# A graph network in one kernel: Householder reflections and bisection steps planned into other LSTM steps

## The reference, cut to what matters

```python
# layer 0: two graph convolutions, then LSTMs over windows of p = 1..4 nodes
h = relu(einsum('ts,bsh->bth', adj, x @ Wg0 + bg0))
h = relu(einsum('ts,bsh->bth', adj, h @ Wg1 + bg1))
for p in range(1, MAX_SKIP + 1):
    nw = Tv // p
    wins = h[:, :nw * p, :].reshape(Bv * nw, p, Hd)
    last = _lstm_last(Wih[p-1], Whh[p-1], bih[p-1], bhh[p-1], wins)
    h = h.at[:, arange(nw) * p + (p - 1), :].set(last.reshape(Bv, nw, Hd))
x = layernorm(x + h)
# layer 1: x -> normalised adjacency -> W1 -> batch norm -> relu -> W2 -> batch norm
# layer 2: attention over 512 edges
# layer 3: spectral, with the eigenvectors U of the normalised Laplacian of adj
_, U = eigh(L_norm)
out = relu(einsum('mn,bnd->bmd', U.T, x) @ W1 + b1) @ W2 + b2
x = layernorm(x + einsum('nm,bmd->bnd', U, out))
```

## Time and profile before

| what | value |
|---|---|
| median of 3 runs | 2091.99 us (2091.33 to 2092.39) |
| the profiled execution | 2091.33 us |
| its span, first to last instruction | 2089.5 us |
| mean granted clock of TensorE | 0.966 of full speed |
| busy: PE, DVE, ACT, POOL | 1948.3, 1493.8, 1144.0, 758.3 us |
| LSTMs: p = 1, 2, 3, 4 | about 228 to 398, 636, 920, 1222 us |

### The profile page before, as it was taken

How to read it: one execution, slowest core, us unless ns; L and a number is a source line. 1 busy time by engine, 2 the same in 40 slices (tenths; PEclk the granted TensorE clock), 3 DMA queues, 4 the chain that set the end, 5 groups by cost and what they waited for, 6 DMA issues and landing times. The chain is left out here.

```text
span 2089.5 us, 32693 instructions
## 1 busy us (share of the span) xinstructions
PE 1948.3 (93%) x11833; PEld 1651.2 (79%) x11833; DVE 1493.8 (71%) x3825; ACT 1144.0 (55%) x1803; POOL 758.3 (36%) x1924
## 2 busy tenths in 40 slices
PE   6999888999999999999999989989799899699996
PEld 6999766788889999988787778866599534469896
DVE  5676666666656677788888878968656489789675
ACT  2444565445444454543444447747567588556675
POOL 2333345443444555000000036646544000107675
PEclk8999998999999999999999999999899999899898
DMA  3110101000100000010000033202222000004022
GB/s 107 47 41 1 41 1 41 1 1 1 41 1 1 1 1 1 1 41 1 1 1 0 1 106 102 91 21 92 69 82 72 11 1 1 11 21 123 32 71 82
DMA packets 65631, 71.15 MB, mean 34 GB/s; under 512 B 3767, under 2 KB 63294, under 8 KB 65470
## 3 DMA queue, kind: packets, MB, share of 16 engines
q1 hardware_dynamic: 65470, 69.07, 10.3%
HBM read 43.90 MB, written 25.17 MB: 33 GB/s over the span
## 5 line engine op out<-in xcount | busy, mean ns | idle before, releaser
L1852 ACT ACTIVATE l_gates<-l_acc,l_b 128x512 f32<-128x512 f32 (+1 forms) x504 | 300.9, 633 | 92.4 <-PE l_acc L473 90.0
L1859 ACT ACTIVATE l_gates<-l_cell 128x512 f32<-128x512 f32 (+1 forms) x144 | 84.0, 583 | 249.8 <-DVE l_cell L1913 156.3
L471 PE MATMUL l_acc<-l_x_hi,l_w1x_hi 128*128 128x336 f32 (+1 forms) x544 | 190.5, 350 | 20.4 <-DVE l_x_lo L1822 12.4
L1812 ACT ACTIVATE l_x_hi<-hT 128x512 fp32r<-128x512 f32 (+1 forms) x144 | 101.0, 755 | 172.4 <-PE l_acc L473 172.4
L473 PE MATMUL l_acc<-l_x_lo,l_w1x_hi 128*128 128x336 f32 (+1 forms) x544 | 190.5, 350 | 0.0
L472 PE MATMUL l_acc<-l_x_hi,l_w1x_lo 128*128 128x336 f32 (+1 forms) x544 | 190.2, 350 | 0.0
L471 PE MATMUL l_acc<-l_x_hi,l_w0x_hi 128*128 128x512 f32 x464 | 182.7, 394 | 6.7 <-ACT l_gates L1852 4.2
L472 PE MATMUL l_acc<-l_x_hi,l_w0x_lo 128*128 128x512 f32 x464 | 181.9, 392 | 0.0
L473 PE MATMUL l_acc<-l_x_lo,l_w0x_hi 128*128 128x512 f32 x464 | 181.8, 392 | 0.0
L183 POOL TENSOR_SCALAR bi_shifted<-bi_shifted 32x1 f32<-32x1 f32 x62 | 36.2, 585 | 400.1 <-DVE bi_shifted L173 400.1
L1243 ACT ACTIVATE leaky<-sc_g 128x1024 f32<-128x1024 f32 x128 | 121.1, 1031 | 21.8 <-PE sc_g L1357 21.4
(11 more groups left out here) (517 smaller groups left out, 6233.2 us busy)
## 6 DMA issues: line engine op xcount, KB each, us to landing
xin<-in_x SPq DMA_DIRECT2D x16, 512.0 KB, 3.9
hidB<-in_x SPq DMA_DIRECT2D x16, 512.0 KB, 4.9
x<-hT SPq DMA_DIRECT2D x16, 512.0 KB, 3.2
hidB<-x SPq DMA_DIRECT2D x16, 512.0 KB, 3.8
x<-hidB SPq DMA_DIRECT2D x16, 512.0 KB, 2.9
attention_residual<-x SPq DMA_DIRECT2D x16, 512.0 KB, 3.9
out_x<-hT SPq DMA_DIRECT2D x16, 512.0 KB, 2.9
l_rawx<-in_wih SPq DMA_DIRECT2D x4, 1024.0 KB, 5.0
```

What stands on the lines that cost most here:

```text
L471: t.matmul(out, left[0], right[0], start=start, stop=False)
L1812: i = nc.scalar.activation(as_windows(xs[s % 2][0][:, ch, 0:bg * nw], nw), cols(p, bg, nw, group, k, ch), ACT.Copy)
L1852: i = a.activation(gates[:, j, q, 0:n], acc[:, j, q, 0:n], FUNC[q], bias=b[:, o:o + 1])
L1859: a.activation(tcell[:, j, 0:n], cell[:, j, 0:n], TANH).then_inc(tc, 1)
```

## The change

The planner puts a reflection into the second unit of k = 0 of the groups 1 to 7 of p = 2, so that the later ones move forward and the bisection begins and ends earlier; the numbers of bisection steps for each unit of p = 4 are other ones, with some behind the last unit of a group. On ScalarE the split of W1 moves from (group 0, k = 3) to (1, 1), and the high part of the first rows from (3, 2) to (2, 2). On GpSimd `y_lo(0)` comes ahead of `params` of group 1 and `params` of group 2 ahead of `y_lo(1)`. What is computed stays the same.

```diff
--- before.py
+++ after.py
@@ -728,13 +728,13 @@
             n1.params(p, pool, 0)
             pool.wait_ge(mat_hi, 1)
             p.tensor_tensor(A[1][:, :], a1, A[0][:, :].bitcast(F32), ALU.subtract).then_inc(mat_lo, 1)
+            y_lo(0)
             n1.params(p, pool, 1)
-            y_lo(0)
             pool.wait_ge(lstm["hidden"], DONE)
             pool.wait_ge(mix, 1)
             set_constants()
+            n1.params(p, pool, 2)
             y_lo(1)
-            n1.params(p, pool, 2)
             for g in range(GROUPS):
                 if g + 3 < GROUPS:
                     n1.params(p, pool, g + 3)
@@ -795,14 +795,14 @@
 
         def beside_scalar(act, group, k, j):
             if k and j:
-                if (group, k) == (0, 3):
+                if (group, k) == (1, 1):
                     act.wait_ge(w_in, 16)
                     nc.scalar.activation(wa[0][:, :], raw_w1, ACT.Copy).then_inc(w_hi, 1)
                 if (group, k) == (2, 1):
                     act.wait_ge(mat_done, 1)
                     nc.scalar.activation(A[0][:, :], a1, ACT.Copy).then_inc(mat_hi, 1)
                     n1.scale(nc.scalar, act, rows(hT, 0), 0)
-                if (group, k) == (3, 2):
+                if (group, k) == (2, 2):
                     y_hi(act, 0)
                 if (group, k) == (3, 1):
                     n1.scale(nc.scalar, act, rows(hT, 1), 1)
@@ -1671,6 +1671,8 @@
                 here = [(u + 1, u + 1, update_last)]
             elif p == 1 and group % 2 == 0:
                 here = [(u, u + 1, update_last)]
+            elif p == 2 and k == 0 and group:
+                here = [(u + 1, u + 1, update_last)]
             elif p in (2, 3) and k:
                 here = [(u, u, update_first)] + ([(u + 1, u + 1, update_last)] if last else [])
             for first, second, table in here:
@@ -1679,7 +1681,7 @@
                     reflection = reflection + 1
                     TRIDIAGONAL = second
             if k and u > TRIDIAGONAL + 1 and reflection == hh.STEPS:
-                many, some, end = (7, 1, 3) if p == 3 else (9 if group == 0 and k < 3 else 12, 2, 0)
+                many, some, end = (7, 1, 3) if p == 3 else (10, 2, 4)
                 if hunted == 0:
                     many = 3
                 for unit, table, n in ((u, hunt_first, many), (u + 1, hunt_first, some)) + (((u + 1, hunt_last, end),) if last else ()):
```

## The result

The changed kernel takes 2146.46 us (median, 2143.7 to 2148.65) against 2091.66 us: a ratio of 1.0261, 95% interval 1.0244 to 1.0279, so 55 us or 2.6% slower (the ratios are worked out from all runs and differ a little from those of the medians). The profiled execution took 2145.22 us. The prediction was 2135, with a range of 2109 to 2154.

A forecast was written before the change was run, and what follows sets the result against it. TensorE was taken to set p = 2 and p = 3, waiting 8.4 us in p = 4, there on DVE's lateness. 2091.3 + 52 - 6 - 2.5 = 2134.8, said as 2135 us, range 2109 to 2154.

The forecast's parts named there:

- Part (a): Seven more reflections in LSTM stretch p = 2, each waiting on GpSimd; p = 2 to grow by 52 us.
- A: In a p = 2 turn, from a group's last Householder column to that in k = 0: 14.4 us, GpSimd's answer 6.7.
- B: Next in the turn, to the column in k = 1, j = 0, DVE only waiting: 8.3 us, GpSimd's answer 5.2.
- C: Last in the turn, to the column behind k = 1, j = 1: 14.1 us, GpSimd's answer 7.7.
- Part (b) in p = 3: Bisection starting in group 3 instead of 6 of p = 3: hidden under TensorE's work, at most 2 us lost.
- Part (b) in p = 4 and the end: Bisection ending earlier in p = 4: 6 us of TensorE waits won there, 2.5 at the hand-over to the convolution.
- part (c): Moves of the W1 split and first convolution rows, and two GpSimd calls exchanged; the exchange priced at nothing.
- the 3.96 us: TensorE's second wait for ax at the hand-over to the convolution, 3.96 us: expected to stay and cover y_lo(1).
- main case: The whole kernel slower through the reflections' stall in p = 2: 2135 us, own range 2121 to 2148, chance 0.72.
- That the reflections fit: Rival for p = 2: the extra reflections cost nothing and only the wins are left, 2083 us; chance 0.07.
- full blocking between DVE and GpSimd: Rival for p = 2: each engine's work wholly stops the other's, 19 us more, 2154 us; chance 0.05.
- TensorE's clock as a rival: Rival for p = 2: waits lower TensorE's clock and it sets the turn again, 2149 us; chance 0.08.

The follow-up runs named there:

- search_as_before: The changed kernel with its seven extra reflections, but the bisection search put back at its old place and numbers; 2140.72 us, ratio 1.0236.
- only_extra_reflections: The kernel before with only the seven extra reflections added, old search numbers and old places of the moved pieces; 2146.35 us, ratio 1.0262.
- no_extra_reflections: The changed kernel without the seven extra reflections, keeping the new search numbers and the moves; 2091.09 us, ratio 1.0001.

## Why the prediction was right, and what it sized wrongly

*Part (a), the mechanism.* Right. Each reflection is a round trip DVE, GpSimd, DVE that the LSTM unit queues behind. Removing the seven brings everything back, adding them alone costs everything, giving TensorE 33 us more work costs nothing, and moving the wait past the cell, with the same work, gives 18 us back.

*Its terms.* The turn was put at A 14.4 + B 8.3 + C 14.1 = 36.8 us; the trace has 14.1 + 8.2 + 14.1 = 36.4. The answers of 5.2, 6.7 and 7.7 us are there, too. Part (a) was to cost 52 us; p = 2 with the stalled end behind it costs 48.6 (42.8 and, from search_as_before, 5.8). One turn could not show that they grow shorter along the stage, from 36.9 us for the first to 35.3 for the last: the seven take 49.5 us more than before, where 52.7 were counted. TensorE's share was put wrong: 7 us idle in two places of a turn, and busy near 80%. It waits in one place, 4 us, and is busy 255.58 of 286.00 (89%); the rest of the stretch went into 14 us of longer busy time at the lower clock.

*Part (b) in p = 3: the step that failed.* "DVE is busy 203.33 of 284.00: hidden, at most 2 us lost." By search_as_before it lost 11.8 us. A mean share says nothing of the single place where DVE is late. The three searches of different weight show that it is the search, and the trace shows where: 2.7 us more at the weight splits, where the search begins at the wrong moment, and 4.1 us in four later waits. That is 7 us of waits, 12.6 against 5.6. The other 5 us are busy time, 287.4 against 282.4 for the same matmuls: the granted clock is 0.92 from 825 to 866 and 0.98 from 866 to 973, where search_as_before has 1.00 from 825 on, and here, where TensorE sets the time, this counts. No run tests this part by itself. With this term at 11.8 instead of nothing the sum would be 2146.6, beside 2145.22 of the profiled execution.

*Part (b) in p = 4 and the end.* 6 and 2.5 us were expected, 3.1 and 2.5 measured (p = 4 from 308.1 to 305.0, the rest from 867.2 to 864.7). The largest wait that is left comes from part (c), which had the W1 split only as leaving the boundary of groups 0 and 1. Its low part on GpSimd now falls on DVE's L1929, which takes 2.72 us instead of 0.69, and TensorE waits 3.50 us for it at 1091.97 (some 2.0 of them are this, by the two lengths), with a granted clock of 0.52 from 1092 to 1098. The kernel before has nothing over 2.1 us in p = 4. With the split at its old place (only_extra_reflections) p = 4 takes 303.8, 1.2 less, but that kernel differs in the search numbers, too. The first c_hid went to 0.45 as predicted. But the 3.96 us did not simply stay: they turned into a 3.22 us wait for y_lo(1), which the prediction had covered by them. The two runs with the old order show that nothing hangs on it. In no_extra_reflections, with the same moves, the l_h_lo of that step is held up as well (2.78 us), but TensorE has no wait there, and p = 4 is 0.5 us shorter than before: what the split costs hangs on what else makes DVE late.

*The whole.* 48.6 + 11.8 - 3.1 - 2.5 is 54.8; p = 1 ended 1.3 us earlier in this execution, which leaves the 53.5 between the two spans. Two errors ran against each other (52 for 48.6, and 6 for 3.1), so that the 11.8 us of p = 3 are nearly the whole difference to 2135. The measured time lies 1.5 us inside the main case's own range (2121 to 2148) with a term of 11.8 us in it that the sum did not have: so the number owes something to the width of the range; the mechanism of part (a) does not.

*The rivals.* That the reflections fit (2083) is out. For full blocking between DVE and GpSimd, chain A would need an answer of 7.7 us and C 9.4; they take 6.6 and 7.7. In chain C of the changed kernel the scalars end 7.05 us behind the column, with 4.0 us of 512-column DVE work beside them, and 4.55 with DVE idle: 0.6 us for each us, as taken. But this price is one for these short pieces: in the turn with the weight splits the scalars end 10.38 us behind the column with 7.0 us of DVE work beside them, 4.4 us more than in another chain A for 4.5 us more work. The Trainium skill, "SBUF — State Buffer", section "Who interferes with whom", has the pair as a lock that fully blocks the loser, and also says that which DVE operations take it depends on their operands; the trace agrees that GpSimd's first two operations are held up (1.21 and 0.86 us) and that L183 takes 5.01 us beside the weight splits, but in a chain with short pieces of DVE work not all of DVE's time is lost to GpSimd. TensorE's clock as a rival was wrong for p = 2: it did fall there, to 0.93, and the run with more TensorE work shows that nothing hangs on it. It seems right where nobody had looked for it, in p = 3, by the 5 us of busy time above.

What stays open: p = 4 with the old search took 308.1, 309.7, 310.1 and 310.2 us in four kernels. TensorE's waits over 0.15 us in it sum to 8.3, 8.6, 10.7 and 9.6 us; why they differ stays open. So does why the later waits of p = 3 need the early search, and what the exchange on GpSimd changes behind the LSTM.

## What to carry to other kernels

Work that is put into an engine's idle time must be asked two things: how long it waits there for another engine, and which queue stands behind that wait. Seven reflections of 3 us DVE work each cost 48.6 us, because each brought a blocking answer of 5 to 8 us; where such a wait stands (behind the cell: 18 us) and what its answer still has to do when DVE is waiting (the basis update: 21 us) gave back about a third of the loss each.

A busy share over a stage doesn't say that more work is hidden. With DVE busy for 65% of p = 3, 20 and 49 more search steps cost 5 and 12 us there, and the trace shows the cost at single places. So look at the single unit, above all where another rare piece of work (here the weight splits) falls due. The same holds for a piece that is moved as free: one instruction of 2.44 us on GpSimd, put beside the wrong one of DVE's, made TensorE wait 3.5 us.

And when a chain is found to set a stage, look for it in the other stages as well: the exchange that mended the changed kernel's p = 2 made the kernel before 0.4% faster, most of it in its p = 1.

## What the runs showed of the hardware

GpSimd loses time to DVE's wide operations, whichever instructions it has then. The same dependent [32 x 1] operation took 0.23 us or 1.21 us (L183), 0.33 or 0.86 (L184), by what DVE did beside it, and scalars that began 0.65 us later ended at the same distance from the column, 5.97 against 5.98 us. With 2.4 and 4.05 us of 512-column work beside the scalars they ended 1.4 and 2.5 us later than with DVE idle. Beside two 2048-column subtractions and a cell product that followed at once, L183 took the whole 5 us; DVE's cell product ended at 541.47:

```profile
536.55 5.01 POOL L183 TENSOR_SCALAR bi_shifted<-bi_shifted 32x1 f32<-32x1 f32 x1 [6.52 <-DVE bi_shifted L173]
```

It goes the other way, too. A GpSimd subtraction of 128 x 1024 elements (L727, 2.44 us) that began 0.26 us ahead of DVE's l_h_lo made that one 2.72 us long instead of 0.69, ending 0.54 behind GpSimd's. The same is seen at y_lo(0) (L725, 2.49 us; l_h_lo 2.77 us at 1189.34).

TensorE came down to 1.2 GHz at waits of about 4 us in p = 2, matmuls of 512 columns then starting 0.43 us apart instead of 0.23, with the stretch at 0.93 of the full clock. With its waits filled by useless matmuls the stretch was at 0.99. In p = 3 waits of 12.6 us in 300 came with 7.6 us more busy time for the same matmuls.
